# A fused adaLN attention and gated FFN block: the gated layer's low weight halves move to GpSimd, and the opening and closing orders are written anew

## The reference, cut to what matters

```
# x: (128 sequences, 32 tokens, 256), cond: (128, 256); 16 heads of 16; FFN width 1024
scale, shift = split(cond @ W_emb + b_emb)
xn   = rms_norm(x, g_norm) * (1 + scale) + shift
q, k, v = split(xn @ W_qkv);  q, k = rms_norm per head
o    = softmax(q k^T / 4) v            # the attention called a
r    = o + o @ W_out                   # residual of the second half
a2   = causal attention of rms_norm(r, ln1) with Wq, Wk, Wv, Wo   # the attention called b
mod  = 0.1 * tanh(a2 @ A)
h    = rms_norm(r, ln2)
gate = silu(h @ W_in^T + mod * (h @ A) @ B)
out  = x + r + (gate * (h @ W_up^T)) @ W_down^T
```

## Time and profile before

| what | value |
|---|---|
| median of 3 runs | 651.57 us (649.97 to 651.59) |
| the profiled execution, own time | 646.44 us |
| its span, first to last instruction | 644.6 us |
| TensorE busy | 600.9 us, 93% of the span |
| VectorE, ScalarE, GpSimd busy | 462.1, 370.0, 221.1 us |
| mean granted TensorE clock | 0.973 of full speed |

### The profile page before, as it was taken

The page is one execution under the profiler, slowest core; times in us unless marked ns, Lnnn a source line. Parts: engine busy times, 40 slices in busy tenths (PEclk is TensorE's granted clock), DMA queues, the critical chain, the costliest instruction groups (busy, mean ns, idle before and its releaser), DMA issues.

```text
span 644.6 us, 22549 instructions
## 1 busy us (share of the span) xinstructions
PE 600.9 (93%) x9112; PEld 558.6 (87%) x9128; DVE 462.1 (72%) x1070; ACT 370.0 (57%) x803; POOL 221.1 (34%) x196
## 2 busy tenths in 40 slices
PE   9565789899999999999999999999999999999997
PEld 8544679788999999999999999999999998888997
DVE  4567878577686777777786767777787766976452
ACT  3647656474565748475665747474656657473531
POOL 1221323415153443424242444334242533523132
PEclk9956799899999999999999999999999999999999
DMA  6322200000201002010101001010101010010000
GB/s 181 90 82 82 71 20 23 14 21 17 67 18 49 19 4 60 11 53 16 50 18 51 19 14 50 8 56 13 51 18 50 18 35 15 7 39 15 27 25 34
DMA packets 31961, 24.35 MB, mean 38 GB/s; under 512 B 7632, under 2 KB 30800, under 8 KB 31872
## 3 DMA queue, kind: packets, MB, share of 16 engines
q1 hardware_dynamic: 31328, 22.36, 11.8%
q10 hardware_dynamic: 544, 0.66, 0.4%
HBM read 14.61 MB, written 4.19 MB: 29 GB/s over the span
## 4 chain that ended last, share of the span: by engine, by line
PE 75%; SPq 10%; DVE 6%; issue 4%; ACT 2%; DMA 2%; POOL 1%; POOLq 0%; ACTq 0%; DVEq 0%
PE gate_bank L494 12%; PE up_bank L494 11%; PE down_bank L718 10%; SPq L469 10%; PE b_banks L494 7%; PE a_banks L486 7%; PE x_bank L486 6%; PE a_banks L609 4%; PE b_banks L486 3%; PE b_banks L506 2%; PE gate_bank L704 2%; PE a_banks L506 2%; PE up_bank L533 2%; DMA vj<-vs 2%; PE b_banks L671 2%
## 5 line engine op out<-in xcount | busy, mean ns | idle before, releaser
L1123 POOL TENSOR_TENSOR gl<-gu,gh 128x512 fp32r<-128x512 f32 x64 | 83.1, 1299 | 117.9 <-ACT gh L877 117.7
L1075 DVE SCALAR_TENSOR_TENSOR th<-th,gate_bank 128x512 f32<-128x512 f32 x64 | 43.2, 675 | 46.8 <-ACT th L872 46.8
L494 PE MATMUL up_bank<-uh,wup_hi 128*128 128x256 f32 x256 | 76.3, 298 | 0.0
L1111 POOL TENSOR_TENSOR qk<-qk,rx 128x512 f32<-128x512 f32 x32 | 33.3, 1060 | 123.6 <-DVE rx L903 123.6
L718 PE MATMUL down_bank<-wdn_hi,gh 128*128 128x256 f32 x256 | 74.1, 290 | 0.6 <-POOL gl L1123 0.6
L494 PE MATMUL gate_bank<-uh,win_hi 128*128 128x256 f32 x256 | 72.4, 283 | 0.2
L718 PE MATMUL down_bank<-wdn_hi,gl 128*128 128x256 f32 x256 | 72.1, 282 | 0.0
L718 PE MATMUL down_bank<-wdn_lo,gh 128*128 128x256 f32 x256 | 72.1, 282 | 0.0
L494 PE MATMUL up_bank<-ul,wup_hi 128*128 128x256 f32 x256 | 71.9, 281 | 0.0
L494 PE MATMUL up_bank<-uh,wup_lo 128*128 128x256 f32 x256 | 71.9, 281 | 0.0
L494 PE MATMUL gate_bank<-ul,win_hi 128*128 128x256 f32 x256 | 71.4, 279 | 0.0
(11 more groups left out here) (157 smaller groups left out, 1844.4 us busy)
## 6 DMA issues: line engine op xcount, KB each, us to landing
xa<-in_x SPq DMA_DIRECT2D x16, 256.0 KB, 3.6
xres<-in_x SPq DMA_DIRECT2D x16, 256.0 KB, 2.9
vj<-vs SPq DMA_DIRECT2D x256, 16.0 KB
out<-outb SPq DMA_DIRECT2D x16, 256.0 KB, 3.2
stage<-in_w_inT SPq DMA_DIRECT2D x2, 512.0 KB, 3.6
stage<-in_w_upT SPq DMA_DIRECT2D x2, 512.0 KB, 4.2
stage<-in_w_downT SPq DMA_DIRECT2D x2, 512.0 KB, 4.0
stage<-in_w_qkv SPq DMA_DIRECT2D x2, 384.0 KB, 4.9
```

What stands on the lines that cost most here:

```text
L494: mm = pe.matmul(dst, w[a][:, k, c0:c0 + P], mov[b][:, k, :], start=(first and k == 0 and j == 0), stop=(last and k == KT - 1 and j == 2), ...
L1075: dve.scalar_tensor_tensor(out=whole, in0=whole, scalar=1.0, in1=Gb[:, :], op0=ALU.add, op1=ALU.mult).then_inc(f_half, 1)
L1111: pool.tensor_tensor(heads_of, heads_of, rx[:, 32 * t:32 * t + 32].unsqueeze(2).to_broadcast([P, 2 * H, HD]), ALU.mult).then_inc(done[name ...
L1123: pool.tensor_tensor(gl[:, c % 2], gu[:, c % 2], gh[:, c % 2].bitcast(F32), ALU.subtract).then_inc(f_lo, 1)
```

## The change

It has six parts.

1. Pieces 6 to 11 (in, up, down) get their low half on GpSimd. The scale used to be applied inside the VectorE instruction; now GpSimd first multiplies the stage in place (in and up only) and then subtracts. So in and up cost it two instructions of 128x1024 each, down costs one. The factor 0.5 moves from the down to the up weights.
2. x_load 0 and 1 come first in the SyncE queue, and the loads of b_emb and g_norm move to the ScalarE queue.
3. x_shift, x_lo, a_scale0 and a_scale1 of block 0, and f_lo3 of block 15, run on VectorE.
4. START and END are replaced by new orders. ORDER is kept. The warm products change in number and place.
5. f_out of block 15 is made in two halves, which two queues store.
6. The counts of the semaphores follow (pool_split beside piece_split).

```diff
+        pool_piece = [name[:2] in ("in", "up", "do") for name in piece_names]
...
-                return [(st, w[0][:, k, :], w[1][:, k, :], small[:, 10 + k:11 + k])]
+                col = (10 if name[:2] == "in" else 14) + k
+                return [(st, w[0][:, k, :], w[1][:, k, :], small[:, col:col + 1])]
...
-                    sp.wait_ge(piece_split, n - 1)
+                    wait_piece(sp, n - 2)
...
+                elif name == "f_store" and last(n, PAIRS - 1):
+                    sp.wait_ge(first_out, 1)
+                    sp.dma_start(outv[n, :, 0, :], outb[odd][:, 0, :]).then_inc(out_stored[odd], 16)
...
+                elif name == "f_store" and last(n, PAIRS - 1):
+                    wait(act, f_out, n)
+                    act.dma_start(outv[n, :, 1, :], outb[odd][:, 1, :]).then_inc(out_stored[odd], 16)
...
+                elif name in ("a_scale0", "a_scale1") and first(n):
+                    t = int(name[-1])
+                    dve.wait_ge(done[f"a_copy{t}"], 1)
+                    dve.wait_ge(done["a_rms"], 1)
+                    heads_of = qk[:, t, :].rearrange("p (h d) -> p h d", d=HD)
+                    dve.tensor_tensor(heads_of, heads_of, rx[:, 32 * t:32 * t + 32].unsqueeze(2).to_broadcast([P, 2 * H, HD]),
+                                      ALU.mult).then_inc(done[name], 1)
...
+                elif name[:4] == "f_lo" and last(n, int(name[4])):
+                    c = int(name[4])
+                    wait(dve, f_hi, n, PAIRS, c + 1)
+                    wait(dve, f_lo, n, PAIRS, c)
+                    dve.tensor_tensor(gl[:, c % 2], gu[:, c % 2], gh[:, c % 2].bitcast(F32), ALU.subtract).then_inc(f_lo, 1)
...
+                if name == "lo" and pool_piece[n]:
+                    pool.wait_ge(piece_hi, n + 1)
+                    for st, hi_ap, lo_ap, scale in piece_parts(n):
+                        if piece_names[n][:4] != "down":
+                            pool.tensor_scalar(st, st, scale, None, ALU.mult).then_inc(piece_scaled, 1)
+                            pool.wait_ge(piece_scaled, sum(pool_piece[:n + 1]))
+                        ins = pool.tensor_tensor(lo_ap, st, hi_ap.bitcast(F32), ALU.subtract)
+                    ins.then_inc(pool_split, 1)
```

More of the change, by code:

```diff
@@ L106 @@
-    ("m_tanh", 1), ("load", 12), ("a_copy0", 3), ("a_copy1", 3), ("m_out", 1), ("f_lo1", 1), ("x_load", 4),
-    ("b_move", 0), ("a_weigh0", 3), ("vd_zero", 0), ("r_square", 2), ("x_norm0", 4), ("x_norm1", 4), ("a_rms", 3),
-    ("f_up2", 0), ("a_v", 2), ("f_gate3", 0), ("r_load", 1), ("x_turn", 3), ("f_down0", 0), ("f_up3", 0),
-    ("b_weigh1", 2), ("f_down1", 0), ("a_pv0", 2), ("a_pv1", 2), ("a_qk1", 3), ("r_rms", 2), ("a_qk0", 3),
-    ("f_half0", 1), ("f_out", 0), ("b_pv", 1), ("x_lo", 4), ("f_down2", 0), ("r_lo", 2), ("f_tanh0", 1),
[13 rows of a table removed]
@@ L124 @@
-    ("b_v1", 2), ("b_q", 2), ("f_gate2", 1), ("a_v", 3), ("a_scale1", 4), ("o_lo", 3), ("m_mul", 2),
-    ("b_scores", 2), ("r_rms", 3), ("a_sum0", 4), ("f_out", 1), ("f_hi0", 2), ("f_half0", 2), ("f_store", 0),
[6 rows of a table removed]
+    ("mt_zero", 0), ("ld_emb", 0), ("first_rms", 0), ("b_emb_one", 0), ("scale_cols", 0), ("lo", 0),
+    ("shift_cols", 0), ("x_scale", 0), ("warm", 8), ("emb_scale", 0), ("ld_b_emb", 0), ("emb_shift", 0),
+    ("x_shift", 0), ("lo", 1), ("x_square", 0), ("x_lo", 0), ("hi", 0), ("x_turn", 0), ("x_norm0", 0),
[9 rows of a table added]
@@ new lines @@
+    ("load", 5), ("r_lo", 0), ("r_add", 0), ("x_scale", 2), ("a_shift1", 1), ("a_shift0", 1), ("b_v_out1", 0),
+    ("a_exp1", 1), ("warm_down", 6), ("a_turn1", 1), ("load", 6), ("b_k_out0", 0), ("a_turn0", 1), ("a_exp0", 1),
+    ("r_turn", 0), ("x_load", 2), ("b_q_out", 0), ("b_k_out3", 0), ("a_rowsum1", 1), ("x_turn", 2), ("b_k", 0),
[3 rows of a table added]
+    ("x_load", 3), ("o_hi", 1), ("a_scores", 1), ("b_v1", 0), ("b_q", 0), ("hi", 11), ("a_v", 1), ("f_up0", 0),
+    ("b_scores", 0), ("a_weigh0", 2), ("x_shift", 3), ("o_even", 1), ("a_pv0", 1), ("hi", 12), ("x_lo", 3),
@@ new lines @@
+    ("a_copy0", 2), ("a_square0", 2), ("a_square1", 2), ("m_tanh", 0), ("a_pv1", 1), ("load", 10), ("a_qk0", 2),
+    ("r_square", 1), ("b_rowsum1", 0), ("m_out", 0), ("f_lo1", 0), ("a_qk1", 2), ("a_copy1", 2), ("r_load", 1),
+    ("b_pv", 0), ("x_norm0", 3), ("r_mm", 1), ("m_turn", 0), ("o_lo", 1), ("b_rowsum0", 0), ("b_flip1", 0),
+    ("lo", 12), ("f_gate0", 0), ("x_norm1", 3), ("f_tanh0", 0), ("b_flip0", 0), ("r_norm0", 1), ("r_norm1", 1),
+    ("a_turn0", 2), ("a_turn1", 2), ("r_turn", 1), ("f_gate1", 0), ("a_k_out3", 2), ("b_k", 1), ("b_v0", 1),
@@ new lines @@
+    ("b_flip1", 2), ("x_scale", 4), ("o_even", 3), ("f_half3", 1), ("x_lo", 4), ("f_down1", 1), ("o_odd", 3),
+    ("f_mul3", 1), ("o_lo", 3), ("f_hi2", 1), ("f_tanh3", 1), ("o_hi", 3), ("f_down2", 1), ("m_mul", 2),
+    ("r_rms", 3), ("f_half0", 2), ("m_tanh", 2), ("r_mm", 3), ("m_turn", 2), ("a_qk0", 4), ("a_qk1", 4),
+    ("f_gate0", 2), ("x_hi", 4), ("f_lo3", 1), ("vd_zero", 0), ("f_out", 1), ("r_turn", 3), ("f_down3", 1),
[5 rows of a table added]
+    ("b_v1", 3), ("b_q", 3), ("b_k_out2", 3), ("f_gate2", 2), ("f_store", 1), ("b_q_out", 3), ("b_scores", 3),
@@ L161 @@
-    ("r_rms", 15), ("f_out", 13), ("f_down3", 13), ("r_lo", 15), ("r_add", 15), ("f_up0", 14), ("o_hi", 15),
[12 rows of a table removed]
-    ("f_out", 14), ("m_tanh", 15), ("f_hi3", 14), ("f_mul1", 15), ("f_store", 15), ("m_out", 15), ("f_tanh0", 15),
[4 rows of a table removed]
[9 rows of a table added]
+    ("a_qk1", 15), ("a_qk0", 15), ("b_pv", 13), ("b_move", 14), ("r_mm", 14), ("m_turn", 13), ("f_up0", 13),
+    ("f_gate0", 13), ("b_weigh0", 13), ("f_lo3", 12), ("a_sum0", 15), ("m_mul", 13), ("a_scale1", 15),
+    ("a_scale0", 15), ("a_exp0", 14), ("a_rms", 15), ("f_tanh3", 12), ("f_down3", 12), ("f_hi2", 12), ("x_hi", 15),
```

126 lines of the change are left out of this document (79 added, 47 removed), and 161 rows, old and new, of tables (END, START).

## The result

The changed kernel takes 667.35 us (median of 5 runs, 665.79 to 667.40). The kernel before, timed beside it, takes 649.97 (646.16 to 651.59). The ratio is 1.0269, with a 95% interval of 1.0231 to 1.0308: slower by 2.7%, three times the forecast of 0.9%, and outside its range. The direction was right. The profiled execution of the changed kernel has a span of 665.5 us, 20.9 longer than the one before. The medians differ by 17.4. The other 3.5 us lie in which execution was profiled: that of the kernel before took 646.44 us, under its median, that of the changed kernel 667.35, its median.

What follows compares the result with a forecast made beforehand. TensorE, busy 395.18 of 400 us in the loop, was taken as the bound. Opening 3 plus closing 2.8 gave 5.8 us lost, so 651.57 + 5.8 = 657.4 us on the median, range 648 to 664.

Steps and rivals of the forecast that it cites:

- Loop: Steady loop: TensorE is busy 395.18 of 400 us, so gains on other engines do not move the end; 0 us.
- Closing: Last blocks: longer b_pv waits of 2.3 and 1.4 us, less 0.6 and 0.3; 2.8 us lost, bounds 0.5 and 5.
- a slow-clock stretch behind the pauses: Closing: TensorE may run at a lower clock after its waits; counted only within the upper bound of 5 us.
- Opening: Start of the kernel: 0 + 4 + 1 - 2 = 3 us lost, bounds 4 gained and 7 lost.
- The first product: Opening: TensorE's first product moves from 17.49 to about 14.6 us, through earlier x and work moved to VectorE.
- For the multiplication I take 1.3: Opening, GpSimd: the new one-input multiplication of 1024 columns takes 1.3 us, bounds 1.0 and 2.6.
- The lock at r_rms.0: Opening, block 0: GpSimd holds VectorE's steps for a_scale's 2.1 and lo.8's 3.9 us; r_rms.0 ends at 56.7.
- The load behind b_move: Opening: load.12 queues behind b_move.0, so b_pv.0 comes 17.6 us after b_v_out1.0 instead of 11.8.
- The wait at b_pv.2: Opening: b_pv.2 has 12.5 us of cover against the 12.8 b_move needs; 1 us lost.
- Tail: End of block 15: f_lo3.15 on VectorE removes 0.6 us before f_down3.15; two half-size stores save 0.3 us.
- Rival 3: GpSimd's instructions slower than doubled, f_up0 and f_down0 wait for pieces, TensorE's clock stays low: 662 to 666 us; chance 0.13.
- Rival 1: The opening's lead survives, decided at r_rms.0 ending by about 51 us: 648.5 us; chance 0.2.

Runs made afterwards that it cites:

- e2: The changed kernel with VectorE's first instruction cut into seventeen, so later VectorE instructions stand 16 places further on; 668.10 us, ratio 1.0293 to the kernel before.
- e4: The changed kernel with the closing order END of the kernel before, the last store put at its end; 658.32 us, ratio 1.0140 to the kernel before.
- e7: The changed kernel with VectorE's first instruction cut into 33, so later ones stand 32 places further on; 661.74 us, ratio 1.0240 to the kernel before.
- e3: The changed kernel with hi.12 moved behind m_tanh.0 on ScalarE and lo.12 behind b_flip0.0 on VectorE; 665.10 us, ratio 1.0235 to the kernel before.
- e10: The kernel before with only f_lo3.15 on VectorE and f_out.15 in two halves stored by two queues, last in END; 646.74 us, ratio 0.9974.
- e12: The changed kernel, VectorE's first instruction cut into 33, without GpSimd's multiplication of in and up pieces (wrong output); 661.66 us, ratio 1.0198 to the kernel before.

## Why the prediction was right in direction and wrong in size

- **Loop, forecast 0 ("nothing gained on another engine there moves the end, and ORDER stays as it is"): wrong by 5.1 us.** This is the step that failed outright, and it had no bound. The order was the same, but VectorE's program ahead of it was not the same length. The argument looked for gains only. A reader of the rows could have seen rr and gl start within 0.01 us of each other in every loop block, with 1.2 us behind the outcome.
- **Closing, forecast 2.8 (bounds 0.5 to 5), measured 8.7.** The waits were read rightly: b_pv.14 waits 2.8 us (forecast 1.3 to 3.1) and b_pv.15 2.0 (forecast 2.3 more). Idle time grew by 4.2. The term that was mis-sized is "a slow-clock stretch behind the pauses": it stood in the bound and not in the sum, and measured 4.5. With it the closing lies above its bound.
- **Opening, forecast 3 (bounds 4 gained to 7 lost), measured 7.1 in one pair of executions and about 4 over all of them.** The sum came out about right, though several terms in it did not. The first product comes at 15.6, not 14.6, since the identity matrix comes late; TensorE then waits 2.6 us for VectorE's a_scale and 2.7 ahead of a_pv. "For the multiplication I take 1.3" (bounds 1.0 and 2.6) measured 2.85, outside its bounds; the subtraction, 2.6, measured 2.38. The lock at r_rms.0 had a_scale's 2.1 as forecast, but 1.05 and not 3.9 for lo.8, and at r_rms.1 lo.11 held a step for 2.27 (forecast 2.6). What was not forecast is that a_rms.1 is held too, for 0.94 and 2.26. r_rms.0 ended at 58.5 (forecast 56.7, bounds 53 and 58), in e2, e4 and e7 at 56.1 to 57.6.
- **The load behind b_move: right to the tenth in this trace.** b_pv.0 comes 17.6 us behind b_v_out1.0 (17.0, 18.0 and 17.8 in e4, e2 and e7). Its worth was less than its length: e3 takes 4.4 us off this way, and at most about 2 are left. The wait at b_pv.2 is 1.6 (forecast 1).
- **Tail: 0.9 forecast, 1.6 in e10's trace.**

By the medians 17.4 us were lost where 5.8 were forecast. Of the 11.6 between them 5.1 are the loop and 5.9 the closing, most of it clock. The prediction also read that nearly all idle time outside the 4.1 us of 100 to 140 and about 3 at the end lay before 100 us. The rows have 27.7 there, 4.8 in the loop and 7.2 in the closing.

Rival 3 (GpSimd slower than doubled, with a slow clock) came nearest in time, and its condition held (2.85 us), but its loss would have come from f_up0 and f_down0 waiting for their pieces, and TensorE's waits in the changed kernel list none for them. Rival 1 died at r_rms.0, which ended well past its turning point of 51.

Two rules of the Trainium skill bear on this. "SBUF — State Buffer", section "SBUF: two separate sides", has the shared pair held for the whole instruction, against VectorE operations with two SBUF inputs or in a 2-port mode. The trace agrees for the two-input subtraction (2.27 of 2.34 us in e12), and not for the one-input multiplication at r_rms.0 (1.05 of 2.85). The step of 0.91 us that the prediction counts for two inputs has only one (TENSOR_SCALAR), so it doesn't bear out that part of the rule. "GPSIMD Engine Reference", section "Engine selection", calls GpSimd slower by about 2 times with two inputs and roughly at line rate with one. The rows have 2.38 us for two inputs (1.9 times the 1.276 of the earlier trace rows). For one input they have 2.85, 2.2 times the same 1.276, so its second half doesn't hold here.
